# Perceiver cross-attention: 32x32 block transposes on VectorE and 32-row score products in place of 128x128 transposes on TensorE

## The chip, the cores and the metric

One core of one Trainium2 chip. The metric is the device time of one execution in microseconds (us); lower is better.

## The reference, cut to what matters

The program is a perceiver layer in three parts: cross-attention over a long context, a gated recurrence, and a mixture of eight experts. Only the first part and the loads at its end are touched.

```python
# x: (32, 64, 512) f32, ctx_1024: (32, 1601, 512) f32, d = 512
def _L0_xattn_ref(encoder_hc, decoder_hq, w_sim, b_sim, W_qv, b_qv):   # hc = layernorm(x), hq = ctx
    Sim = (hc @ w1)[:, :, None] + (hq @ w2)[:, None, :] + einsum('bid,bjd->bij', hc * w3, hq) + b_sim[0]
    hq_hat = einsum('bij,bjd->bid', softmax(Sim, axis=2), hq)
    Batt = softmax(max(Sim, axis=2), axis=1)
    hc_bar = einsum('bi,bid->bd', Batt, hc)[:, None, :]
    feats = concatenate([hc, hq_hat, hc * hq_hat, hc * hc_bar], axis=-1)
    return feats @ W_qv + b_qv
x = x + _L0_xattn_ref(_layernorm(x), ctx_1024, ...)
x = x + recurrence(...)      # unchanged
x = x + experts(...)         # unchanged
```

## The kernel before, in words

**Tiling.** The 32 batches go in 16 pairs; a pair's 2 x 64 query rows fill the 128 partitions. A batch's context has 1601 rows: 12 tiles of 128 and one of 65. Tiles 0 to 5 have two buffers (`ctx_two`, one of them lying in `x2`), tiles 6 to 12 one (`ctx_one`).

**Stages of a pair.** The normalised x (`tok_rows`) is turned on TensorE (L361) into `hcT`. VectorE makes the queries `qT = hcT * w3 + w2` (L619). Each context tile is turned by four 128x128 transposes on TensorE (`turn_ctx`, L353) into a PSUM bank T, batch 0's into T[0] and batch 1's into T[1]. ScalarE drains T[0] and VectorE T[1] into `ctxT` (`drain_ctx`, L487). The score product (`scores`, L390) contracts 128 features at a time in four steps, the batches on the two halves of the array's columns, into the PSUM banks S. VectorE takes each bank's maximum (L694), ScalarE the exponentials (L554). TensorE turns the probabilities (`turn_probs`, L371), and both engines drain them into `probsT`. The value product (L425) multiplies them with the untransposed context. Last comes the output product into Y: 12 matmuls with `hqhH/hqhL` (L396 to L398), 8 with `wb` and `hcT` (L458), 12 with `f2H/f2L`. VectorE adds Y to `xb` (L577). A side branch turns `tcol`, the row maxima (L417), makes the second softmax in one partition (L601 to L629), spreads it with one matmul (L431), and from it VectorE makes `hcb` (L637, L641); GpSimd then makes `wb` in four instructions (L327, L331).

**Order.** Every engine runs one `body(p, s, step)` a step (`steps`): the back half of pair p (values and output) with the front half of pair p + 1 (scores and softmax). On TensorE a body is: the 13 positions of the value product in `AV_ORDER`, with the first block of context transposes, the turn of `tok_rows` and that of `tcol` between them; the five score blocks of `BLOCKS`, the transposes of the next block put between the four contraction steps; the output product, with the turns of the probabilities in it. `turn_order` counts, for the waits, whose turn it is on T[0] and T[1].

```python
for c in range(C):                                              # scores, L384 to L391
    if j + 1 < NBLK and c < BLOCKS[j + 1][1]:
        turn_ctx(j + 1, 2 * c, p, fs, loads, step)
        turn_ctx(j + 1, 2 * c + 1, p, fs, loads, step)
    for b in range(2):
        last = pe.matmul(S[64 * b:64 * b + 64, k, col:col + w], qT[:, c, 64 * b:64 * b + 64],
                         buf[:, b, c, 0:w], start=(c == 0), stop=(c == C - 1))
```

**Queues.** SyncE issues all loads. In `step` it waits for each block of `ctx_one` to be read by the value product (`av_one`) and loads it again for the next pair (L241, L244), then stores the last x1 (L278), then loads x (L232) and both `ctx_two` blocks. GpSimd's `xb` (L318) waits for the store before last. ScalarE issues no DMA in this part.

An f32 matmul that is no transpose is two records in the trace, with two weight loads; an f32 transpose and an `fp32r` matmul are one.

Of the kernel before, what the change touches and what calls it, by code (L numbers as in the profile page):

```python
# [5 lines left out]
F32 = mybir.dt.float32  # L6
# [8 lines left out]
P = 128  # L15
# [28 lines left out]
BLOCKS = [(0, 3, 0, 0), (3, 3, 1, 0), (6, 3, 2, 0), (9, 2, 3, 0), (11, 2, 3, 256)]  # L44
NBLK = len(BLOCKS)
BANK_TILES = [(0, 3), (3, 3), (6, 3), (9, 4)]


TWO_SLOTS = 2
AV_ORDER = [t for j in [*range(TWO_SLOTS, NBLK), *range(TWO_SLOTS)] for t in range(BLOCKS[j][0], BLOCKS[j][0] + BLOCKS[j][1])]  # L50
AT_TILES = [(0, 4), (4, 3), (7, 3), (10, 3)]


def turn_order(front, back):

    bank = ([], [])
    for j, (_, n, _, _) in enumerate(BLOCKS):
        for u in range(2 * n if front else 0):
            bank[u % 2].append(f"ctx{j}.{u}")
    if front:  # L60
        bank[0].insert(1, "hc")
    if back:
        bank[1].insert(1 if front else 0, "trow")
# [30 lines left out]
def cross_attention(nc, sh, ident, x, ctx, w_sim, b_sim, W_qv, b_qv, x1, x2, ahead):  # L94
    D, C, JT, JMAIN, JTAIL, PAIRS = sh.D, sh.C, sh.JT, sh.JMAIN, sh.JTAIL, sh.PAIRS
    BW = 3 * P
    sems = []

    with ExitStack() as stack:
# [6 lines left out]

        TWO = BLOCKS[TWO_SLOTS][0]

        ctx_two = [[x2[:, b * TWO:(b + 1) * TWO, :] for b in range(2)], [sb(f"ctx_two{b}", [P, TWO, D]) for b in range(2)]]
        ctx_one = [sb(f"ctx_one{b}", [P, JT - TWO, D]) for b in range(2)]  # L110
        ctxT = [sb(f"ctxT{s}", [P, 2, C, BW]) for s in range(2)]
        w0, w3 = x2[:, 2 * TWO:2 * TWO + C, :], sb("w3", [P, C, D])
# [5 lines left out]
        qT = sb("qT", [P, C, P])  # L118
        probs = sb("probs", [P, JT * P])
        probsT = sb("probsT", [P, JT, P])  # L120
        hqhH, hqhL = sb("hqhH", [P, C, P], F32R), sb("hqhL", [P, C, P], F32R)
        wb = sb("wb", [P, 2, C, D])
        f2H, f2L = sb("f2H", [P, C, P], F32R), sb("f2L", [P, C, P], F32R)
# [10 lines left out]
        rstd = sb("rstd", [P, 1])  # L134
        mhalf = sb("mhalf", [P, 1])
        s1 = sb("s1", [P, 1])
        mx4 = sb("mx4", [P, 4])
        mx = sb("mx", [P, 1])
        nmx = sb("nmx", [P, 1])
        z4 = sb("z4", [P, 4])  # L140
# [9 lines left out]
        hcb = sb("hcb", [P, C, 2])  # L150

# [8 lines left out]
        hqhH_ready, hqhL_ready, f2H_ready = sem("hqhH_ready"), sem("hqhL_ready"), sem("f2H_ready")  # L160
        x_in = sem("x_in")
        ctx_in = [[sem(f"ctx_in{s}_{j}") for j in range(TWO_SLOTS)] for s in range(2)]
        ctx_one_in = [sem(f"ctx_one_in{j}") for j in range(TWO_SLOTS, NBLK)]
# [5 lines left out]
        rstd_ready = sem("rstd_ready")  # L169
        hc_ready = sem("hc_ready")  # L170
        xb_ready = sem("xb_ready")
        q_ready = sem("q_ready")
# [16 lines left out]
        f2_ready = sem("f2_ready")  # L189
# [3 lines left out]
        y_done = sem("y_done")  # L193
# [5 lines left out]
        def tile_rows(t):  # L199
            return P if t < JT - 1 else JTAIL  # L200

        def bank_cols(k):
            t0, n = BANK_TILES[k]
            return sum(tile_rows(t) for t in range(t0, t0 + n))

        def context(s, b, t):

            return (ctx_two[s][b], t) if t < TWO else (ctx_one[b], t - TWO)

        def block_dmas(j):  # L210
            t0, n, _, _ = BLOCKS[j]
            return 2 * (2 if t0 + n == JT else 1)

        def block_cols(j):
            t0, n, _, _ = BLOCKS[j]
            return sum(tile_rows(t) for t in range(t0, t0 + n))

        def steps(eng, body):

            body(-1, 0, "first")  # L220
            body(0, 0, "full")
            with eng.Fori(0, (PAIRS - 2) // 2) as i:
                body(2 * i + 1, 1, "full")
                body(2 * i + 2, 0, "full")
            body(PAIRS - 1, 1, "last")
# [4 lines left out]
        def _(sp):  # L230
# [3 lines left out]
            def load_block(j, s, pair):  # L234
                t0, n, _, _ = BLOCKS[j]
                done = ctx_in[s][j] if j < TWO_SLOTS else ctx_one_in[j - TWO_SLOTS]
                for b in range(2):
                    src = ctx[pair, b]
                    dst, i = context(s, b, t0)
                    full = min(n, JT - 1 - t0)  # L240
                    sp.dma_start(dst[:, i:i + full, :],  # L241
                                 src[0:JMAIN, :].rearrange("(p t) d -> p t d", t=JT - 1)[:, t0:t0 + full, :]).then_inc(done, 16)
                    if full < n:
                        sp.dma_start(dst[0:JTAIL, i + full, :], src[JMAIN:sh.J, :]).then_inc(done, 16)  # L244
# [8 lines left out]
            for j in range(NBLK):  # L253
                load_block(j, 0, 0)
# [9 lines left out]
            for j in range(TWO_SLOTS):  # L264
                load_block(j, 1, 1)

            def step(p, s, load, store):
                nxt = p + 1 if isinstance(p, int) else sp.snap(p + 1)
                if load:
                    ahead = p + 2 if isinstance(p, int) else sp.snap(p + 2)  # L270
                if store:
                    prev = p - 1 if isinstance(p, int) else sp.snap(p - 1)
                for j in range(TWO_SLOTS, NBLK):
                    sp.wait_ge(av_one, (NBLK - TWO_SLOTS) * p + j - TWO_SLOTS + 1)
                    load_block(j, None, nxt)
                if store:
                    sp.wait_ge(x1_ready, p)
                    sp.dma_start(x1[prev], xb[1 - s][:]).then_inc(x1_out, 16)  # L278
                if load:
                    sp.wait_ge(hc_ready, p + 2)  # L280
                    sp.wait_ge(xb_ready, p + 2)
                    load_x(ahead)
                    sp.wait_ge(av_done, p + 1)
                    for j in range(TWO_SLOTS):
                        load_block(j, s, ahead)
# [10 lines left out]
            ahead.load(sp)  # L296
# [7 lines left out]
        def _(pool):  # L304
            pool.memset(mhalf[:], -0.5).then_inc(consts, 1)
            pool.memset(ones1[:], 1.0).then_inc(consts, 1)
            pool.wait_ge(consts, 2)
            pool.wait_ge(const_in, 80)

            def body(p, s, step):  # L310

                if step != "last":
                    f = p + 1
                    pool.wait_ge(ln_ready, 2 * f + 2)
                    pool.tensor_tensor(rstd[:], ve[:], mhalf[:], ALU.pow).then_inc(rstd_ready, 1)  # L315
                    if not (isinstance(f, int) and f < 2):
                        pool.wait_ge(x1_out, 16 * (f - 1))
                    pool.tensor_tensor(xb[1 - s if step != "first" else 0][:], x_sb[:], bqv_b[:], ALU.add).then_inc(xb_ready, 1)  # L318
                if step != "first":
# [6 lines left out]
                    for b in range(2 if step == "full" else 0):  # L326
                        pool.tensor_tensor(wb[:, b], w3[:], hcb[:, :, b, None].to_broadcast([P, C, D]),  # L327
                                           ALU.mult).then_inc(wb_step, 1)
                    for b in range(2 if step == "full" else 0):
# [3 lines left out]
            steps(pool, body)  # L333

        @block.tensor
        def _(pe):
# [3 lines left out]

            def turn_ctx(j, u, p, fs, loads, step):

                t0, n, _, _ = BLOCKS[j]
                t, b, bank = t0 + u // 2, u % 2, u % 2
# [1857 lines left out]
```

## Time and profile before

| | |
|---|---|
| median of 3 runs | 1582.35 us (1582.21 to 1584.47) |
| span of the profiled execution | 1606.2 us |
| TensorE matmul busy | 1417.7 us, 88% |
| TensorE weight loads busy | 914.6 us, 57% |
| VectorE busy | 721.5 us, 45% |
| ScalarE busy | 377.6 us, 24% |
| GpSimd busy | 756.1 us, 47% |
| cross-attention | from the start to about 842 us |
| mean granted TensorE clock | 0.947 of 2.4 GHz |

The profiled execution has only its span: 1606.2 us from the first to the last instruction, 1.5% over the median of the unprofiled runs. Busy time of TensorE is the time covered by at least one matmul whose end is modelled, so matmuls that run side by side or pipelined count once. Shares of the whole span mix the three parts of the program; the cross-attention has to be read by itself.

### The profile page before, as it was taken

To read this page: it belongs to the slowest core of one execution; us is meant where nothing else is said; L and a number is where in the kernel's file an instruction comes from. 1 tells how busy PE (TensorE), PEld (TensorE's weight loads), DVE (VectorE), ACT (ScalarE), POOL (GpSimd) and SP (SyncE) were. 2 spreads that over 40 slices of the span, in tenths; PEclk is the share of its full clock that TensorE was granted. 3 is DMA by queue.
4 is the path that set the end of the run, shared out by engine and by line. 5 is a ranking of instruction groups with operands and counts; after the bars stand their busy time and mean duration, and the time that the engine had idled before them with its cause. 6 is when DMAs were issued, how large, how long until landed. Compare 5 with 4: busy or idle time off the path is not lost. (4 is left out here: it accounts for less than half of the span.)

```text
span 1606.2 us, 28597 instructions
## 1 busy us (share of the span) xinstructions
PE 1417.7 (88%) x9329; PEld 914.6 (57%) x9330; DVE 721.5 (45%) x1715; ACT 377.6 (24%) x716; POOL 756.1 (47%) x592
## 2 busy tenths in 40 slices
PE   5899999999999999999998777898549999996960
PEld 3455555555555555555546556666438888885750
DVE  2443434434344344443437776787583233231221
ACT  1322222322223222232215412222301111111110
POOL 0134431444214442144406855787495886806830
PEclk9999999999999999999998999999679999998985
DMA  9514542244422444224406569532103333314322
GB/s 331 191 53 147 177 177 92 107 154 176 172 96 99 162 176 161 107 92 169 170 7 224 165 242 318 176 111 97 66 27 131 137 137 131 139 57 144 117 67 103
DMA packets 94905, 225.10 MB, mean 140 GB/s; under 512 B 9448, under 2 KB 25960, under 8 KB 94864
## 3 DMA queue, kind: packets, MB, share of 16 engines
q1 hardware_dynamic: 85136, 191.02, 34.0%
q0 software_dynamic: 9200, 32.51, 5.8%
q10 hardware_dynamic: 528, 1.05, 0.2%
q8 instruction: 23, 0.38, 0.1%
q14 instruction: 18, 0.15, 0.0%
HBM read 179.20 MB, written 45.35 MB: 140 GB/s over the span
## 5 line engine op out<-in xcount | busy, mean ns | idle before, releaser
L487 DVE COPY ctxT<-T 128x512 f32<-128x512 f32 (+1 forms) x208 | 139.6, 671 | 251.4 <-PE T L353 251.4
L487 ACT COPY ctxT<-T 128x512 f32<-128x512 f32 (+1 forms) x208 | 118.7, 570 | 450.0 <-PE T L353 450.0
L390 PE MATMUL S<-ctxT,qT 128*64 128x384 f32 (+2 forms) x1280 | 211.7, 448 | 0.0
L318 POOL TENSOR_TENSOR xb<-x_sb,bqv_b 128x512 f32<-128x512 f32 x16 | 20.3, 1272 | 256.9 <-DMA x<-xb 256.9
L331 POOL TENSOR_TENSOR wb<-wb,x 128x2048 f32<-128x2048 f32 x30 | 135.5, 4538 | 0.0
L353 PEld LDWEIGHTS T<-ident,ctx_one 128*128 128x128 f32 (+1 forms) x896 | 92.0, 141 | 63.6 <-ACT ctxT L487 34.9
L315 POOL TENSOR_TENSOR rstd<-ve,mhalf 128x1 f32<-128x1 f32 x16 | 8.8, 551 | 252.7 <-DVE nmean L573 252.7
L353 PE MATMUL T<-ident,ctx_one 128*128 128x128 f32 (+1 forms) x896 | 116.9, 273 | 0.0
L327 POOL TENSOR_TENSOR wb<-w,hcb 128x2048 f32<-128x2048 f32 x30 | 107.5, 3606 | 19.1 <-DVE w12L L646 19.1
L1881 POOL TENSOR_TENSOR w_high<-w_low,f_zero 128x2048 fp32r<-128x2048 f32 x21 | 96.8, 4609 | 36.3 <-DMA w_low<-_L_ffn_gate_up_proj_dram 24.7
L1932 PE MATMUL f_Dn<-w_high,f_hH 128*128 x156 | 67.9, 435 | 49.6 <-issue 48.0
L425 PE MATMUL O<-ctx_one,probsT 128*64 128x512 f32 (+1 forms) x448 | 110.9, 611 | 0.0
L390 PEld LDWEIGHTS S<-ctxT,qT 128*64 128x64 f32 x1280 | 76.4, 136 | 57.4 <-issue 49.7
L1862 POOL TENSOR_TENSOR w_low<-w_low,w_high 128x2048 fp32r<-128x2048 f32 x21 | 96.7, 4606 | 1.6
L1398 PE MATMUL Pb<-WrT,yT 128*32 128x128 f32 x2016 | 71.8, 286 | 22.2 <-DVE yT L1633 20.1
L2037 DVE TENSOR_TENSOR f_hL<-f_TH,f_hH 128x512 fp32r<-128x512 f32 x39 | 27.0, 691 | 140.3 <-ACT f_hH L1987 140.3
L1992 ACT ACTIVATE sg<-f_G 128x512 f32<-128x512 f32 x39 | 23.4, 599 | 244.8 <-PE f_G L1934 212.6
L1398 PEld LDWEIGHTS Pb<-WrT,yT 128*32 128x32 f32 x2016 | 53.7, 113 | 33.4 <-DVE yT L1633 28.9
L353 PEld LDWEIGHTS T<-ident,x 128*128 128x128 f32 x384 | 45.1, 149 | 45.6 <-ACT ctxT L487 14.3
L353 PE MATMUL T<-ident,x 128*128 128x128 f32 x384 | 56.2, 293 | 16.5 <-DMA x<-in_ctx_dram 13.3
L458 PE MATMUL Y<-wb,hcT 128*64 128x512 f32 x256 | 65.1, 610 | 0.0
L1932 PE MATMUL f_U<-w_high,f_xH 128*128 x156 | 64.9, 416 | 0.0
(299 smaller groups left out, 2925.0 us busy)
## 6 DMA issues: line engine op xcount, KB each, us to landing
x<-in_ctx_dram SPq DMA_DIRECT2D x32, 768.0 KB, 7.3
ctx_one<-in_ctx_dram SPq DMA_DIRECT2D x32, 768.0 KB, 5.6
ctx_two<-in_ctx_dram SPq DMA_DIRECT2D x32, 768.0 KB, 7.3
ctx_one<-in_ctx_dram SPq DMA_DIRECT2D x32, 512.0 KB, 5.4
w_low<-_L_ffn_gate_up_proj_dram POOLq DMA_DIRECT2D x10, 1024.0 KB, 8.3
f_xt<-routed_x SPq DMA_DIRECT2D x39, 256.0 KB
routed_y<-f_yt SPq DMA_DIRECT2D x39, 256.0 KB
ctx_one<-in_ctx_dram SPq DMA_DIRECT2D x32, 256.0 KB
```

The lines of the kernel that those rows point to most:

```text
L327: pool.tensor_tensor(wb[:, b], w3[:], hcb[:, :, b, None].to_broadcast([P, C, D]), ALU.mult).then_inc(wb_step, 1)
L331: pool.tensor_tensor(wb[:, b], wb[:, b], w0, ALU.add).then_inc(wb_step, 1)
L353: last = pe.transpose(T[bank][:, c * P:c * P + rows], src[0:rows, i, c * P:(c + 1) * P], ident[0:rows, 0:rows])
L390: last = pe.matmul(S[64 * b:64 * b + 64, k, col:col + w], qT[:, c, 64 * b:64 * b + 64], buf[:, b, c, 0:w], start=(c == 0), stop=(c == C - 1))
L425: last = pe.matmul(O[64 * b:64 * b + 64, :], probsT[0:rows, t, 64 * b:64 * b + 64], src[0:rows, i, :], start=(n == 0), stop=(n == JT - 1))
L458: pe.matmul(Y[64 * b:64 * b + 64, :], hcT[s][:, c, 64 * b:64 * b + 64], wb[:, b, c, :], start=False, stop=False)
L487: copy(buf[:, bank, :, i * P:i * P + rows], T[bank][:].rearrange("p (c j) -> p c j", c=C)[:, :, 0:rows]).then_inc(t_free[bank], 1)
L1398: last = pe.matmul(Pb[o * B:(o + 1) * B, 0:P], src[:, c, prev, :], WrT[:, c, o * P:(o + 1) * P], start=(c == 0), stop=(c == C - 1))
L1862: pool.tensor_tensor(low, low.bitcast(F32), high[:, e % SLOTS, part].bitcast(F32), ALU.subtract).then_inc(w_parts, 1)
L1881: pool.tensor_tensor(high[:, e % SLOTS, part], ex.low[:, e % SLOTS, part].bitcast(F32), zero[:, None, :].to_broadcast([P, C, F]), ALU.add) ...
L1932: pe.matmul(bank[:], aH[:, c, :], high[:, slot, part, c, :], start=(c == 0), stop=False)
L2037: dve.tensor_tensor(hL[:], TH[:].rearrange("p (c i) -> p c i", c=C), hH[:].bitcast(F32), ALU.subtract).then_inc(hL_ready, 1)
```

## The change

What it does:

- The context transposes on TensorE, their drains and `ctxT` go. VectorE transposes the context from SBUF to SBUF in blocks of 32x32 (`dve.transpose`), two tiles of one batch an instruction, into `ctxA` (positions 0 to 3, later 9 to 12) and `ctxB` (4 to 8; its space also holds `probs`). Only the blocks are turned: partition group a (32 partitions) of the result holds, for each of 16 groups of 32 features, the features of tokens 32a to 32a + 31.
- A score matmul contracts 32 features: 16 steps k, for each batch the four partition groups a in turn, each with its own PSUM bank. It needs the queries with every feature group on all four partition groups (`qr`). ScalarE makes the queries into `f3`, writes them to DRAM (`q_rows`), waits, and reads them back in four DMAs.
- Three score blocks of 4, 5 and 4 positions in place of five. The row maximum is taken once at the end (three reductions), the exponentials in five instructions.
- The normalisation goes to ScalarE, at the end of the body before, and `hc` is turned ahead of the values. The two `f` operands share buffers (`hfH`, `hfL`). The output product's first 12 matmuls come ahead of the last score block.
- SyncE stores x1 first and loads x between the second and third part of `ctx_one`. The last two full bodies stand outside the loop. The load of `Wg` waits for the last scores.

```diff
+BLOCKS = [(0, 4, 0), (4, 5, 8), (9, 4, 4)]
+TAIL_POS = 8
+AV_ORDER = [*range(4, 13), *range(0, 4)]
+PARTS_ONE = [(4, 2, False), (6, 2, True), (8, 2, False), (10, 2, False)]
+PART_ENDS = [1, 4, 6, 8]
...
             def step(p, s, load, store):
...
+                    sp.wait_ge(x1_ready, p)
+                    sp.dma_start(x1[prev], xb[1 - s][:]).then_inc(x1_out, 16)
+                for i in range(len(PARTS_ONE)):
+                    if i == 2 and load:
+                        sp.wait_ge(hc_ready, p + 2)
+                        sp.wait_ge(xb_ready, p + 2)
+                        load_x(after)
+                    sp.wait_ge(av_one, len(PARTS_ONE) * p + i + 1)
+                    load_part(i, nxt)
                 if load:
                     sp.wait_ge(av_done, p + 1)
+                    load_two(s, after)
...
+            def scores(j, f):
+                t0, n, col = BLOCKS[j]
+                buf = (ctxA, ctxB)[j % 2]
+                pe.wait_ge(turned[j], f + 1)
                 if j == 0:
+                    pe.wait_ge(q_in, 64 * (f + 1))
+                    pe.wait_ge(exp_done, EXPS * f)
+                for k in range(DB):
+                    c, e = k // QUADS, k % QUADS
                     for b in range(2):
+                        for a in range(QUADS):
+                            w = n * Q
...
+                            last = pe.matmul(S[64 * b:64 * b + 64, a, col * Q:col * Q + w], qr[a * Q:(a + 1) * Q, e, c, 64 * b:64 * b + 64],
+                                             buf[a * Q:(a + 1) * Q, b, k, 0:w], start=(k == 0), stop=(k == DB - 1))
...
# body on TensorE, after the change: hc turn; values(p); scores(0); hqh turn; scores(1);
# 12 matmuls with hfH/hfL; scores(2); 8 with wb, turn_probs(0) in them; 12 with hfH/hfL, turn_probs(1 to 3) in them
...
# ScalarE, each body
+                    for c in range(C):
+                        act.activation(f3[:, c, :], hcT[fs][:, c, :], ACT.Identity, scale=w3T[:, c:c + 1],
+                                       bias=w2T[:, c:c + 1]).then_inc(q_made, 1)
+                    act.wait_ge(q_made, C * (f + 1))
+                    if later(f, 1):
+                        act.wait_ge(q_in, 64 * f)
+                    act.dma_start(q_d, f3[:].rearrange("p c i -> p (c i)")).then_inc(q_out, 16)
+                    act.wait_ge(q_out, 16 * (f + 1))
+                    if later(f, 1):
+                        act.wait_ge(qk_done, NBLK * f)
+                    for a in range(QUADS):
+                        act.dma_start(qr[a * Q:(a + 1) * Q].rearrange("p e c i -> p e (c i)"),
+                                      q_d.rearrange("(e r) d -> r e d", r=Q)).then_inc(q_in, 16)
...
# VectorE
+            def turn_two(buf, src, i, b, col):
+                return dve.transpose(buf[:, b, :, col * Q:(col + 2) * Q].rearrange("p k (t r) -> p t k r", r=Q),
+                                     src[:, i:i + 2, :].rearrange("p t (k r) -> p t k r", r=Q))
...
+            def row_max(f):
+                full, end = JTAIL // Q, (JT - 1) * Q
+                dve.wait_ge(qk_done, NBLK * (f + 1))
+                dve.tensor_reduce(mx3[:, 0:1], S[:, 0:full, 0:end + Q], axis=AX.XY, op=ALU.max).then_inc(mx_done, 1)
+                dve.tensor_reduce(mx3[:, 1:2], S[:, full:QUADS, 0:end], axis=AX.XY, op=ALU.max).then_inc(mx_done, 1)
+                dve.tensor_reduce(mx3[:, 2:3], S[:, full, end:end + JTAIL % Q], axis=AX.X, op=ALU.max).then_inc(mx_done, 1)
...
# VectorE's body after the change: add_x; second softmax; f3, hcb (wait q_out); s1; turn_second;
# norm_stats; hqhL; f3; turn_third; hfL; row_max; tcol; half of turn_first for the next pair;
# drain_probs 0 and 2; the other half of turn_first; zsum, rz
```

## Rows read from the trace of the kernel before

**Rows 1.** The page: the span, and the busy time and share of the engines.
```profile
span 1606.2 us, 28597 instructions
PE 1417.7 (88%) x9329; PEld 914.6 (57%) x9330; DVE 721.5 (45%) x1715; ACT 377.6 (24%) x716; POOL 756.1 (47%) x592
```

**Rows 2.** Windows: busy us (instructions) of PE, PEld, DVE, ACT, POOL; clock, DMA share, GB/s.
```profile
57.00:815.60 758.60, 755.93 (x4495) 399.85 (x4494) 315.26 (x701) 202.89 (x421) 268.27 (x89) 1.00 0.39 140
262.00:312.40 50.40, 50.37 (x303) 26.72 (x302) 20.85 (x48) 13.48 (x29) 17.93 (x6) 1.00 0.38 141
281.00:291.00 10.00, 10.00 (x68) 5.54 (x66) 3.84 (x6) 3.52 (x6) 10.00 (x3) 1.00 0.89 338
```

**Rows 3.** Timeline, PE: start us, us; the value product's start in two bodies, and others.
```profile
261.98 1.08 PE L425 MATMUL O<-ctx_one,probsT 128*64 128x512 f32 x4
...
264.70 1.09 PE L353 MATMUL T<-ident,ctx_two 128*128 128x128 f32 x8
265.72 1.08 PE L425 MATMUL O<-ctx_one,probsT 128*64 128x512 f32 x4
...
267.75 3.66 PE L425 MATMUL O<-ctx_one,probsT 128*64 128x512 f32 x16
...
312.38 1.08 PE L425 MATMUL O<-ctx_one,probsT 128*64 128x512 f32 x4
```

**Rows 4.** Groups of PE, busy us, mean ns: one body's (262.0 to 312.4); L390's, the page's.
```profile
L458 PE MATMUL Y<-wb,hcT 128*64 128x512 f32 x16 | 4.1, 611 | 0.0
L371 PE MATMUL T<-ident,probs 128*128 128x128 f32 x12 | 2.1, 287 | 0.0
L390 PE MATMUL S<-ctxT,qT 128*64 128x384 f32 (+2 forms) x1280 | 211.7, 448 | 0.0
```

**Rows 5.** Timeline, PE: 32 matmuls of the recurrence, four column groups of the array in turn.
```profile
1000.32 1.08 PE L1398 MATMUL Pb<-WrT,yT 128*32 128x128 f32 x32
```

**Rows 6.** Groups of DVE by form: the recurrence's block transpose; one body's copy and reductions.
```profile
L1633 DVE STREAM_TRANSPOSE yT<-H 128x128 f32<-128x128 f32 x64 | 19.9, 311 | 2.2
L487 DVE COPY ctxT<-T 128x512 f32<-128x512 f32 x12 | 8.3, 692 | 14.9 <-PE T L353 14.9
L694 DVE TENSOR_REDUCE mx<-S 128x1 f32<-128x384 f32 x3 | 1.6, 547 | 0.0
```

**Rows 7.** Groups of ACT by form in the same body.
```profile
L554 ACT ACTIVATE probs<-S,nmx 128x384 f32<-128x384 f32 x3 | 1.7, 578 | 0.4 <-DVE nmx L676 0.4
L554 ACT ACTIVATION_READ_ACCUMULATOR probs<-S,nmx 128x1 f32 x4 | 0.8, 203 | 0.0
L522 ACT ACTIVATE erow<-erow 1x128 f32<-1x128 f32 x1 | 0.3, 303 | 0.0
```

**Rows 8.** DMA issues: count, KB each, median us from issue to landing; one issue's length.
```profile
x_sb<-in_x_dram SPq DMA_DIRECT2D x16, 256.0 KB, 2.6
x<-xb SPq DMA_DIRECT2D x16, 256.0 KB, 5.8
...
281.08 0.33 SPq L232 DMA_DIRECT2D x_sb<-in_x_dram  x1
```

**Rows 9.** Timeline, POOL, in the same body.
```profile
280.81 7.17 POOL L327 TENSOR_TENSOR wb<-w,hcb 128x2048 f32<-128x2048 f32 x2
287.94 9.03 POOL L331 TENSOR_TENSOR wb<-wb,x 128x2048 f32<-128x2048 f32 x2
```

**Rows 10.** Timeline, PE, in the last body; [idle before <-what ended it].
```profile
828.65 0.66 PE L361 MATMUL T<-ident,tok_rows 128*128 128x128 f32 x4 [0.79 <-ACT tok_rows L535]
830.80 0.76 PE L396 MATMUL Y<-w12H,hqhH 128*128 128x512 f32 x1 [1.49 <-DVE hqhL L667]
...
832.21 0.63 PE L396 MATMUL Y<-w12H,hqhH 128*128 128x512 f32 x1
832.64 0.63 PE L397 MATMUL Y<-w12L,hqhH 128*128 128x512 f32 x1
```

**Rows 11.** Timeline, PE, at the start: first score product and first value product.
```profile
25.25 1.55 PE L390 MATMUL S<-ctxT,qT 128*64 128x384 f32 x4
...
57.03 1.97 PE L425 MATMUL O<-ctx_one,probsT 128*64 128x512 f32 x4
```

More of the change, by code:

```diff
@@ L197, in first, with tile_rows, context, part_dmas @@
             return isinstance(p, int) and p == 0
[L199 to L225, printed above, removed]
+        def tile_rows(pos):
+            return JTAIL if pos == TAIL_POS else P
+        def context(s, b, pos):
+            if pos < TWO:
+                return ctx_two[s][b], pos
+            if pos == TAIL_POS:
+                return ctx_one[b], ONE - 1
+            return ctx_one[b], pos - TWO - (pos > TAIL_POS)
+        def part_dmas(i):
+            return 2 * (2 if PARTS_ONE[i][2] else 1)
+        def bodies(eng, body):
+            body(-1, 0, "first", 1)
+            body(0, 0, "full", 2)
+            with eng.Fori(0, (PAIRS - 4) // 2) as i:
+                body(2 * i + 1, 1, "full", i + 2)
+                body(2 * i + 2, 0, "full", i + 3)
+            body(PAIRS - 3, 1, "full", PAIRS // 2)
+            body(PAIRS - 2, 0, "full", None)
+            body(PAIRS - 1, 1, "last", None)
         block = stack.enter_context(nc.Block())
@@ new lines, in values @@
+            def values(p, s, step):
+                pe.wait_ge(hqh_ready, p)
+                for n, pos in enumerate(AV_ORDER):
+                    for q in range(len(AT_TILES)):
+                        if AT_TILES[q][0] == n:
+                            pe.wait_ge(t_free[q % 2], turn(q % 2, f"probs{q}", *before(p)) + 1)
+                    if n == 1:
+                        pe.wait_ge(tcol_ready, p + 1)
+                        fill(1, "trow", p, step)
+                        pe.transpose(T[1][0:1, 0:P], tcol[:], ident[:]).then_inc(t_full[1], 1)
+                    for b in range(2):
+                        rows = tile_rows(pos)
+                        src, i = context(s, b, pos)
+                        last = pe.matmul(O[64 * b:64 * b + 64, :], probsT[0:rows, n, 64 * b:64 * b + 64],
@@ L512, in body @@
                 if front:
-                    drain_ctx(act, copy, 0, 0, p, fs, step, only=(0,))
                     act.wait_ge(t_full[0], turn(0, "hc", p, step) + 1)
@@ L560, in _ @@
+            act.wait_ge(const_in, 80)
+            norm(0)
+            bodies(act, body)
         @block.vector
@@ new lines, in turn_second @@
+            def turn_second(f):
+                dve.wait_ge(ctx_one_in[0], 16 * part_dmas(0) * (f + 1))
+                for b in range(2):
+                    turn_two(ctxB, ctx_one[b], 0, b, 0)
+                dve.wait_ge(ctx_one_in[1], 16 * part_dmas(1) * (f + 1))
+                for b in range(2):
+                    turn_two(ctxB, ctx_one[b], 2, b, 2)
+                for b in range(2):
+                    op = dve.transpose(ctxB[0:96, b, :, 4 * Q:5 * Q], ctx_one[b][0:96, ONE - 1, :].rearrange("p (k r) -> p k r", r=Q))
+                op.then_inc(turned[1], 1)
@@ L656, in body @@
                 if front:
[L657 to L661 removed]
+                    turn_second(f)
+                if loads is not None:
+                    norm_stats(f + 1)
                 if back:
                     dve.wait_ge(hqhH_ready, p + 1)
[L665 removed]
```

446 lines of the change are left out of this document (204 added, 242 removed).

## The prediction, made before the changed kernel had run

> **What bounds the kernel now.** I read the page first [rows 1]: TensorE is busy 88% of the span, but that mixes three parts of the program. The windows are next [rows 2]: from 57 to 815.6 us TensorE is busy 755.9 of 758.6 us at full granted clock (2.4 GHz), while VectorE has 42% and GpSimd 35%. The DMA engines have 39%, and move 338 GB/s at 89% where they work. Then the timeline for the period: the value product starts at 261.98 and again at 312.38 [rows 3], so a body takes 50.4 us, and fifteen start at that pace. In this part only fewer or denser TensorE instructions make the time shorter, until something else takes over.
>
> What fills 50.4 us: the transposes at L353 come eight a time; eight begin at 264.70 and the values resume at 265.72 [rows 3], so one costs 1.02 / 8 = 0.128 us with its share of the switch to and fro. There are 13 tiles x 4 x 2 = 104: **13.3 us**. Scores: 211.7 us in 16 pairs [rows 4] = **13.2 us**. Values: 16 records (4 positions) in 3.66 - 0.2 us of modelled tail = 3.46 [rows 3], so 13 positions take 11.3 us. The L458 products take 4.1 and the turned probabilities 2.1 [rows 4]. The remainder, 50.4 - 13.3 - 13.2 - 11.3 - 4.1 - 2.1 = 6.4 us, is the 24 `fp32r` matmuls and the small turns.
>
> **Part by part.** *Transposes on TensorE*: gone, -13.3 us a body. Their drains (26 copies, up to 0.69 us [rows 6]) were beside them and are worth nothing by themselves.
>
> *Scores.* The columns streamed stay the same if the four partition groups stream at once: 16 steps of 416 columns against 4 steps of 1601. The present product costs 13.2 us with its switches to transposes. From the recurrence: 32 records of 128 columns, four column groups, in 1.08 us [rows 5]; less the 0.27 us of the last one's tail, 0.81 / 8 = 0.10 us a round of four. Its four tiles differ in columns; the new product has eight tiles, four partition groups by two halves of the columns, of which no row shows the partition groups. If all eight go together, a round of 128 columns costs 0.10 to 0.11 us whoever is in it; 16 steps x 2 records x 0.109 x 416/128 = **11.3 us**. Bounds: 11 us below (nothing streams the columns faster), 4 x 11.3 = 45 us above (partition groups one after another). I take the lower end, because the nearest row shows four tiles in the time of one.
>
> The Trainium skill ("TensorE: Matmul & The Clock Gate", Part 3) gives four row tiles of 512 columns as 3.07 times one, not 4; by that the scores would be 45 / 3.07 = 14.7 us, an estimate, and the body 3.4 us longer than I say. No row here shows it.
>
> *Context on VectorE.* One block transpose of 128 elements takes 0.311 us [rows 6]; a copy of 512 takes 0.69. On the line through these, 0.99 ns an element over 0.18 us, 1024 elements cost 1.20 us and 512 cost 0.69. Twelve and two of them: 15.8 us a body. Bounds: half of it, if SBUF to SBUF ran at twice the pace (8 us), and double, if the scattered output cost as much again (32 us, which would put VectorE near 43 us and make it the bound); I take the line, since one of its two rows is the same operation. VectorE has 20.9 us a body now [rows 2]; the drains (9) and the queries (1.1) go, so 27 us with the new small ones: covered, if it is not late.
>
> *Row maximum and exponentials.* Today three of four banks are reduced while scores run. After: 1248 elements on the same line (1.4 us), 384 (0.55 us [rows 6]), and three small ones with their waits: 2.6 us after the last score. ScalarE's first exponential then takes 0.7 with 0.2 for the accumulator [rows 7]. TensorE has only six of the eight L458 matmuls (3.1 us) to put beside these 3.6 us, then waits on the third and fourth exponential. I put **+1.5 us** on the path (0.5 to 3).
>
> *Queries through DRAM.* With the values' start at 0: `hcT` copied at 1.2, second softmax's exponential at 2.9, four activations by the 0.303 us row [rows 7] to 4.1, the write's issue 0.33 [rows 8], its landing between 2.6 and 5.8 us later (the two 256 KB rows [rows 8]), then four issues one behind the other (1.4 us) and 1 MB of reads: 2.6 us at best, more behind the `ctx_one` parts that SyncE issues from 2.5 us on. At 338 GB/s [rows 2] 1 MB alone is 3.1 us. So `qr` is full between 11 and 21 us; TensorE wants it after the values and two small turns, at 12.5. I take 15: **+2.5 us** (0 to 8). ScalarE is blocked meanwhile; behind it stands only the scaling of O, due at 12.5. VectorE's wait for `q_out` holds `hcb` to about 9 us: GpSimd's chain of 7.17 + 9.03 us [rows 9] ends at 25.5, and its product is wanted near 30: hidden, with 5 us to spare.
>
> *VectorE's order.* `turn_second` runs 9.5 to 16, with `hqhL` at 20.5 behind the turn of `tok_rows` after the first score block, `turn_third` to 26; TensorE reaches the third block at 27. Free, barely; each us on VectorE beyond that comes onto the path.
>
> *Ends of the body.* The normalisation (0.7 us) now follows the last drain on ScalarE: **+0.6 us** before `hc` is turned. SyncE's x load waits for `xb`, that for the x1 store (5.8 us [rows 8]): parts 3 and 4 start near 9.5 and land by 18, wanted at 21. The moved store, load of Wg and unrolled bodies: nothing, 15 us and more of slack or the same work.
>
> *Clock.* After idle stretches of 0.79 and 1.49 us in the last body, an `fp32r` matmul starts 0.43 us behind the one before it [rows 10], against at most 6.4 / 24 = 0.27 in the full bodies: the lower level, 1.2 GHz, for some 3 us. The new wait of 2.5 us can bring that on in each body: **+1 us** (0 to 3).
>
> Sum: 50.4 - 13.3 - (13.2 - 11.3) = 35.2, + 1.5 + 2.5 + 0.6 + 1 = 40.8; with 1.2 us for switches between the 32-row tiles and the rest (0 to 2; bound by the switch share above) **42 us a body**, 8.4 saved, times 15 = 126 us. *Start*: the first score comes at 25.25, the first value at 57.03 [rows 11], 32 us; after, two transposed parts and 11.3 us of scores, tied to VectorE's 15.8 us and the landing context, end near 45: 12 us saved. 1606.2 - 138 = 1468 of the profiled span. That span is 1.5% above the median; times 0.985 it is **1446 us**.
>
> **Rivals.** *(A) The forecast*, 37 to 45 us a body: 1372 to 1490. *(B) The queries come 5 us later still* (small packets beside 4 KB ones): 47 us a body, 1520. For it, the 5.8 us row; against, the DMA engines stand idle half the body. *(C) Matmuls never start denser than in the densest stretch of this trace*, 0.81 / 31 = 0.026 us apart [rows 5]: 768 records x 0.026 = 20 us; the body is 50 us and only the start gains: 1570, within 30 either way. For it: no stretch here is denser. Against: there the streaming of the columns explains the pace fully. By a sentence of the same page (Part 1) starts never come closer than 25 ns, which would make the scores 19.2 us; the row at 26 ns neither refutes nor needs it. *(D) The slower side: partition groups of one half of the columns stream one after another.* Scores cost up to 45 us, the body 34 longer less the waits it covers (some 4): 72 us. 1606.2 + 15 x 21.6 - 12 = 1918, times 0.985 = 1890. It decides from scores of about 20 us on, less than two groups at once. For it: only column groups are seen together in the trace, and two records of the same product must follow each other; against: the groups have their own partitions and PSUM banks, and one batch's four are issued together. *(E) VectorE the bound* at doubled transposes is inside B's time or C's.
>
> **Numbers.** A 0.55, B 0.12, C 0.13, D 0.20 (its milder forms included). A and B are faster; C falls to faster 0.06, same 0.03, slower 0.04. So faster 0.73, same 0.03, slower 0.24. 0.2%, about 3 us, is what a measurement of this kernel can tell from no change. The range takes in A, B and the faster half of C: 1370 to 1585; what is left out is D above. A's own is 1372 to 1490.
>
> **What would show it.** Right: value products start 40 to 44 us apart; L353 gone; each score block busy near 3.5, 4.4, 3.5 us; block transposes near 1.20 us; before the first score block a wait for `qr`'s DMA of 2 to 3 us; a wait of TensorE on `probs` near 1 us. Wrong: score blocks of 6 us (C) or 14 us (D); block transposes of 2 us; a wait for `qr` over 6 us (B); `wb` as a releaser.

## The result, and the profile after

The change makes the kernel slower: 1719.43 us (median of 4, 1715.72 to 1721.39) against 1582.28 us beside it, a ratio of 1.0868 (95% interval 1.0849 to 1.0887). The forecast was 1446 us, range 1370 to 1585: the sign and the range were both missed.

The page of the changed kernel, against [rows 1]; under it its transposes, its DMA queues and its issues.

```profile
span 1716.9 us, 46419 instructions
PE 1246.2 (73%) x18673; PEld 884.3 (52%) x18674; DVE 860.1 (50%) x1619; ACT 301.2 (18%) x636; POOL 767.4 (45%) x610
q10 hardware_dynamic: 12048, 22.03, 4.3%
q8 instruction: 135, 2.21, 0.5%
L393 PE MATMUL S<-ctxA,x 32*64 32x128 f32 x8192 | 166.3, 317 | 256.5 <-DMA x<-q_rows 172.4
L593 DVE STREAM_TRANSPOSE ctxA<-ctx_one 128x1024 f32<-128x1024 f32 x64 | 73.9, 1212 | 13.7 <-PE S L393 13.7
ctx_one<-in_ctx_dram SPq DMA_DIRECT2D x128, 512.0 KB, 9.7
x<-q_rows ACTq DMA_DIRECT2D x64, 256.0 KB, 11.0
```

TensorE did what was asked: 1246 us busy where it had 1418. But it has gone from 88% to 73% of its span, and one wait stands out, that of L393 for the queries read back from DRAM. The instruction queue q8 moved 135 packets; in the kernel before, its line reads "q8 instruction: 23, 0.38, 0.1%".

The windows of one body, against the middle line of [rows 2]: values, the stretch behind them, the rest.

```profile
429.60:441.50 11.90, 11.90 (x56) 3.83 (x55) 4.85 (x9) 2.43 (x6) 2.79 (x2) 1.00 0.76 255
441.50:455.40 13.90, 0.39 (x2) 0.00 (x0) 9.32 (x12) 0.69 (x1) 13.90 (x4) 0.70 1.04 323
455.40:488.00 32.60, 28.06 (x829) 21.91 (x829) 15.65 (x22) 5.58 (x16) 1.80 (x3) 0.92 0.08 31
```

TensorE is idle for the whole middle stretch, with the DMA engines full. The timeline of PE, of the same body, against [rows 3]:

```profile
429.59 1.08 PE L417 MATMUL O<-ctx_one,probsT 128*64 128x512 f32 x4
...
438.29 3.60 PE L417 MATMUL O<-x,probsT 128*64 128x512 f32 x16
455.42 1.99 PE L393 MATMUL S<-ctxA,x 32*64 32x128 f32 x61 [13.53 <-DMA x<-q_rows]
...
467.29 2.16 PE L393 MATMUL S<-ctxB,x 32*64 32x129 f32 x115 [1.59 <-issue]
...
472.33 4.09 PE L393 MATMUL S<-ctxA,x 32*64 32x128 f32 x256
477.89 2.79 PE L460 MATMUL Y<-wb,hcT 128*64 128x512 f32 x12 [1.48 <-issue]
...
488.00 1.08 PE L417 MATMUL O<-ctx_one,probsT 128*64 128x512 f32 x4
```

The value products of the sixteen pairs start from 71.5 to 953.8 us, so a body takes 882.3 / 15 = 58.8 us; before, from 57.0 [rows 11] at 50.6. That is 14.5 us at the start and 15 x 8.25 = 123.7 us after it, 138 in all: the whole loss (137) lies in the attention. (The two profiled spans differ by 111 us only: from the last pair's value product to the end the trace before has 791 us and the trace after 763, the difference that chips show below.) Below, a body is always this mean over fifteen, and a block's time runs from its first matmul's start to its last one's, as a mean over fourteen bodies. A wait before a block is counted from the start of the matmul before it, so that some 0.5 us of it is that matmul itself; in the rows, the time in brackets is idleness alone. The three score blocks take 6.0, 6.4 and 4.8 us, 17.3 in place of 11.3, and block 0 starts 26.7 us after the values where the forecast's terms give 12.5 + 2.5 + 0.6 = 15.6. 11 + 6 = 17 us is the gap between 58.8 and the forecast 42.

Where the queries lose their time: ScalarE's timeline, then the group of transfers of `q_rows` in this body, then the DMA of 442 to 453 us.

```profile
431.75 1.63 ACT L517 ACTIVATE f<-hcT,w2T,w3T 128x128 f32<-128x128 f32 x4
433.49 0.35 ACTq L522 DMA_DIRECT2D q_rows<-f  x1
438.56 1.91 ACTq L527 DMA_DIRECT2D x<-q_rows  x4
```
```profile
DMA to landing us min/median/max: 5.0/9.8/15.4
```
```profile
q1 hardware_dynamic: 630, 2.44, 72.4%
q10 hardware_dynamic: 532, 0.99, 31.9%
```

The write leaves 3.9 us after the values start, as forecast (4.1), and needs 5.0 us, inside its bounds. The reads are issued from 9.0 us on, and the last lands 15.4 us after its issue. The third fence says why: SyncE's queue q1, which has ten context transfers of 6 MB under way, and ScalarE's q10 get through nearly as many packets (630 and 532), but q1's hold 3.9 KB and q10's 1.9 KB, so 72% of the bytes are context. The queries' megabyte moves at 90 GB/s. The Trainium skill ("DMA: Bandwidth & Descriptors", Queues, rings and completion order) says that a DMA engine goes round its queues packet by packet; the counts of packets in this window agree with that.

### The profile page after: what moved, and what is told of

Its sections match the earlier page's. It is cut to its first block and busy times, and to the rows that moved or that the text cites. A ratio compares the mean times of both kernels' runs of the same rounds, so it can differ in the third digit from the quotient of the medians.

```text
span 1716.9 us, 46419 instructions
## 1 busy us (share of the span) xinstructions
PE 1246.2 (73%) x18673; PEld 884.3 (52%) x18674; DVE 860.1 (50%) x1619; ACT 301.2 (18%) x636; POOL 767.4 (45%) x610
## 5 line engine op out<-in xcount | busy, mean ns | idle before, releaser
L393 PE MATMUL S<-ctxA,x 32*64 32x128 f32 x8192 | 166.3, 317 | 256.5 <-DMA x<-q_rows 172.4
L393 PEld LDWEIGHTS S<-ctxA,x 32*64 32x64 f32 x8192 | 151.3, 155 | 282.5 <-issue 281.9
L417 PE MATMUL O<-ctx_one,probsT 128*64 128x512 f32 (+1 forms) x576 | 135.8, 606 | 0.0
L393 PE MATMUL S<-ctxB,x 32*64 32x160 f32 (+2 forms) x4096 | 83.4, 296 | 26.1 <-issue 26.1
L393 PEld LDWEIGHTS S<-ctxB,x 32*64 32x64 f32 x4096 | 70.5, 132 | 37.0 <-issue 36.8
L593 DVE STREAM_TRANSPOSE ctxA<-ctx_one 128x1024 f32<-128x1024 f32 x64 | 73.9, 1212 | 13.7 <-PE S L393 13.7
L593 DVE STREAM_TRANSPOSE ctxB<-ctx_one 128x1024 f32<-128x1024 f32 x64 | 73.8, 1207 | 0.0
L417 PEld LDWEIGHTS O<-ctx_one,probsT 128*64 128x64 f32 (+1 forms) x576 | 37.3, 137 | 62.4 <-issue 58.6
L551 ACT ACTIVATE ctxB<-S,nmx 128x512 f32<-128x512 f32 (+2 forms) x80 | 41.0, 528 | 146.1 <-DVE nmx L639 146.1
L1976 PE MATMUL f_Dn<-w_low,f_hH 128*128 x156 | 62.7, 402 | 0.0
## 6 DMA issues: line engine op xcount, KB each, us to landing
x<-in_ctx_dram SPq DMA_DIRECT2D x16, 1024.0 KB, 15.4
```

What stands on the lines that cost most here:

```text
L393: last = pe.matmul(S[64 * b:64 * b + 64, a, col * Q:col * Q + w], qr[a * Q:(a + 1) * Q, e, c, 64 * b:64 * b + 64], buf[a * Q:(a + 1) * Q, ...
L417: last = pe.matmul(O[64 * b:64 * b + 64, :], probsT[0:rows, n, 64 * b:64 * b + 64], src[0:rows, i, :], start=(n == 0), stop=(n == JT - 1))
L593: return dve.transpose(buf[:, b, :, col * Q:(col + 2) * Q].rearrange("p k (t r) -> p t k r", r=Q), src[:, i:i + 2, :].rearrange("p t (k r) ...
L1976: pe.matmul(bank[:], aH[:, c, :], ex.low[:, slot, part, c, :], start=False, stop=False)
```

## The experiments

Chips differ: the kernel before took 1606 us on the chip of the first four runs, 1604 on that of the next four, 1582 on that of the last three. Ratios are to it on the same chip. The difference lies behind the attention: from the last value product on, the eight kernels of the first two chips take 782 to 792 us, the three of the last one 762 to 766, as the changed kernel's first trace does (763). So the bodies may be compared across chips; the changed kernel's takes 58.8 us in one trace and 59.2 in `again`.

**hold.** Parts 2 to 4 of `ctx_one` and x are loaded only when the queries have landed.

```diff
-                    if i == 2 and load:
+                    if i == 1 and load:
                         sp.wait_ge(hc_ready, p + 2)
+                        sp.wait_ge(q_seen, p + 2)
                         sp.wait_ge(xb_ready, p + 2)
...
+                    act.wait_ge(q_in, 64 * (f + 1))      # ScalarE, behind its four reads
+                    act.sem_inc(q_seen, 1)
```


> The changed kernel, but SyncE loads x and the second, third and fourth part of ctx_one only after the queries' four reads have landed (ScalarE waits for them and signals). Theory T1 (the reads are late because they share the DMA engines with the context loads: 15 us of landing against 3 to 4 alone): qr is full about 13 us after the values start, TensorE's wait before the first score block falls from 13.5 us to under 2, the body from 59 to 46 to 48 us, the time to about 1550. Rival R1 (the round trip is long by itself: a chain of write, wait, four issues and reads): the reads still end past 20 us, the body stays over 54 us, the time over 1640.

Measured: ratio 1.0533 (1.0513 to 1.0554), 1691.75 us, a body of 55.2 us: neither side's forecast of the whole holds. The queries' last packet comes 14.5 us after the values' start, not 25.6, and block 0's wait falls from 15 to 3.7 us. PE's timeline of a body whose values start at 404.20:

```profile
419.22 5.61 PE L394 MATMUL S<-ctxA,x 32*64 32x128 f32 x256 [2.72 <-DMA x<-q_rows]
424.76 0.66 PE L366 MATMUL T<-ident,tok_rows 128*128 128x128 f32 x4
430.00 5.09 PE L394 MATMUL S<-ctxB,x 32*64 32x160 f32 x141 [4.59 <-DVE ctxB L619]
```

So some 11 of the 15 us are the sharing. But 11 us earlier queries gave back only 3.6 us a body: block 1 now waits 5.6 us for the context that was held, and the blocks themselves grew to 19.0 us. With `hold`, 14.5 us is what the round trip costs with the engines nearly to itself: the forecast's 15 was the price of an undisturbed trip.

**local.** No DRAM: ScalarE and VectorE each copy eight 32x512 pieces of `f3` to the four partition groups of `qr`.

```diff
-                    act.dma_start(q_d, f3[:].rearrange("p c i -> p (c i)")).then_inc(q_out, 16)
...
-                        act.dma_start(qr[a * Q:(a + 1) * Q].rearrange("p e c i -> p e (c i)"),
-                                      q_d.rearrange("(e r) d -> r e d", r=Q)).then_inc(q_in, 16)
+                    for e in range(2):                    # VectorE: e in range(2, 4)
+                        for a in range(QUADS):
+                            act.copy(qr[a * Q:(a + 1) * Q, e], f3[e * Q:(e + 1) * Q]).then_inc(q_in, 1)
```


> The changed kernel, but the queries don't go through DRAM: ScalarE and VectorE copy f3 onto the four partition groups of qr in eight 32-row copies each. T1: no DMA before the first score block; its wait under 1 us; the low clock after it gone, so the first block takes 5 us instead of 6.3; the body 45 to 47 us; the time about 1525. Rival R2 (VectorE, with 5 us of copies more, becomes the bound): the body 52 us or more, TensorE waiting for the block transposes before the second or third score block.

Measured: 1561.7 us, ratio 0.9731 (0.9714 to 0.9749), faster than the kernel before. A body takes 47.3 us, a little over the 45 to 47 expected, and block 0 isn't waited for (0.5 us, the matmul before it). Everything else in the change stays. But the blocks take 18.3 us (5 us were expected of the first, it takes 5.7), though nothing delays block 0 and block 1 waits only 1.6 us for its operands.

**order.** The column halves of one partition group are issued in turn, not the four groups of one half.

```diff
-                    for b in range(2):
-                        for a in range(QUADS):
+                    for a in range(QUADS):
+                        for b in range(2):
```


> The changed kernel with the two inner loops of the score product swapped: the partition groups outside, the batches inside. Theory T3 (all eight tiles of a step go together whatever their order, as the trace after shows eight starts in 50 ns and then 109 ns to the next eight): the same within 5 us. Rival R3 (the order decides which tiles overlap): score blocks longer or shorter by over 1 us each, the time by over 20 us either way.

Measured: ratio 1.0973 (1.0947 to 1.1), a body of 59.1 us, blocks 6.1, 6.3 and 5.1 us. The body is that of `again` below (59.2 us), but it was profiled in the fastest of the four runs. The ratio is above both of the unedited kernel's (1.0868, and 1.0903 in `again`) by more than the intervals, 11 to 17 us; no unedited run stands beside it on this chip. So the new order gains nothing, the traces show no block longer or shorter by 1 us, and whether it costs up to 1 us a body stays open.

**half.** Scores over 8 of the 16 feature groups; half of the contraction is left out (the last step kept closes the sum).

```diff
-                for k in range(DB):
+                for k in range(DB // 2):
```


> The changed kernel with only 8 of the 16 feature groups in the score product (half of the contraction is left out). Theory T2 (the score blocks take 17 us a body instead of 11.3 because instructions come too slowly, in 16 KB fetches every 3.6 us, now that the loop is too long to stay where it is held): per matmul the supply stays the bound, if the loop of some 160 KB is still fetched each time: blocks of 3.1, 3.3 and 2.5 us, fetches go on. If the shorter loop is held, no fetches in the loop and blocks at the streaming pace: 1.8, 2.2 and 1.8 us. Rival R4 (the blocks are slow for another reason, the clock or the tiles): half the time of the present blocks whether fetches are there or not.

```profile
q8 instruction: 87, 1.43, 0.4%
```

Measured: 1616.02 us (one run), a body of 50.7 us. The blocks take 3.3, 2.4 and 1.8 us, 7.6 in all, less than half of 17.3, near the forecast's pace of 1.8, 2.2 and 1.8 but for block 0, whose rounds all run at half clock (213 ns). The wait for the queries stays at 15.5 us. The instruction packets go on, about 5 a body (57 from 250 to 850 us), some 3.9 us apart in the scores. The expectation tied the streaming pace to packets that are gone; here both come together, so packets as such don't cost. A block is now 256 TensorE instructions, about one packet's worth, and in fourteen bodies a single gap is left in the blocks, of 0.65 us.

**again.** The changed kernel unedited, on the chip of the next three.

> The changed kernel once more, nothing edited, as the yardstick of the kernels beside it. Every theory expects the ratio of the first timing within its interval, 1.085 to 1.089, 58.8 us a body, and block 0 waiting about 15 us for its queries.

Measured: ratio 1.0903 (1.0866 to 1.094), overlapping the first timing's interval, a body of 59.2 us, block 0's wait 15.1 us.

**early.** `local`, with the product that makes `s1` ahead of the one that releases GpSimd.

```diff
+                        score_bias(f)                    # the tensor_tensor_reduce into s1
+                        dve.wait_ge(s1_ready, f + 1)
                     dve.tensor_tensor(f3[:], hcT[s][:], Y[:, None, 0:P]
...
-                    dve.tensor_tensor_reduce(out=f3[:]..., accum_out=s1[:]).then_inc(s1_ready, 1)
```


> The kernel with local query copies, and in it VectorE's product with two SBUF operands that makes s1 moved ahead of the product that releases GpSimd, so that GpSimd is idle while it runs. T4 (such an instruction doesn't end while GpSimd works: it took 4.06 us beside GpSimd's first product against 0.68 us in the kernel before): it takes 0.7 us again, the transposes of block 1 begin and end about 3.4 us earlier, block 1's gap of 1.7 us behind block 0 is gone, and a body takes 1.5 to 3 us less than 47.3, so 1510 to 1540 us on this chip. R5 (the 4 us are the instruction's own, for its operands' places or its form in the changed kernel): it still takes 4 us, GpSimd starts 4 us later, and a body takes 47.3 us or up to 3 more.

The product's group in `local` and in `early` (VectorE, all sixteen):

```profile
L690 DVE CUSTOM_DVE_ANT_0 f<-tok_rows,w_b 128x512 f32<-128x512 f32 x16 | 58.2, 3635 | 2.6 <-DVE hcb L679 2.6
```
```profile
L653 DVE CUSTOM_DVE_ANT_0 f<-tok_rows,w_b 128x512 f32<-128x512 f32 x16 | 11.1, 692 | 26.3 <-ACT x L525 26.1 <-DVE x L644 0.2
```

The instruction's 3.4 us were GpSimd's, as expected; the body's gain was not. It takes 47.4 us, the ratio is 0.9715 (0.970 to 0.973) against 0.9731 for `local`: no difference that the intervals show. Block 1's operands are there 3.5 us sooner, its gap is gone, and the time reappears inside block 1 (8.7 us after 7.9). PE in a body of `early`:

```profile
359.74 2.39 PE L394 MATMUL S<-ctxA,x 32*64 32x128 f32 x146
363.64 1.86 PE L394 MATMUL S<-ctxA,x 32*64 32x128 f32 x110 [1.51 <-issue]
365.43 0.66 PE L366 MATMUL T<-ident,tok_rows 128*128 128x128 f32 x4
366.01 0.51 PE L394 MATMUL S<-ctxB,x 32*64 32x160 f32 x13
369.94 6.19 PE L394 MATMUL S<-ctxB,x 32*64 32x129 f32 x243 [3.41 <-issue]
```

"<-issue" is idle time for which no semaphore answers. The DMA records have an instruction packet of 16 KB that starts at 361.30 and one at 367.45, each beside such a gap.

**narrow.** All but the first feature group write half of their columns; the instructions stay.

```diff
+                            w = w // 2 if k else w
```


> Of the score products all but those of the first feature group write only half of their columns (64 in place of 128, 16 in place of 32): half of the sum is left out of the other columns; the number of instructions stays. T2 (blocks are bound by the supply of TensorE's instructions, 8.3 ns each, and by gaps beside the fetches): the three blocks take nearly what they took, 5.5, 6.0 and 4.5 us or at most 1 us less, fetches as many as before. R6 (streaming of columns bounds them): they fall to half, near 3.2, 3.3 and 2.5 us.

Measured: 1756.07 us (one run; `again` beside it 1748.66), a body of 60.1 us. The blocks take 5.8, 5.7 and 5.2 us, 16.7 in place of 17.4, for nearly half of the streaming. Block 2 of one body, where the changed kernel has one row of 4.09 us:

```profile
479.76 1.70 PE L394 MATMUL S<-ctxA,x 32*64 32x128 f32 x129
482.64 1.58 PE L394 MATMUL S<-ctxA,x 32*64 32x64 f32 x127 [1.19 <-issue]
```

The clock differs too. The windows of this body, block 0 with the start of block 1, and block 2 (the clock is the third number from the end):

```profile
464.20:472.00 7.80, 6.49 (x288) 5.86 (x292) 0.01 (x1) 0.59 (x1) 0.92 (x3) 0.50 0.22 87
479.70:484.30 4.60, 3.34 (x257) 3.13 (x257) 0.73 (x2) 0.62 (x1) 0.00 (x0) 1.00 0.03 7
```

Block 0 runs at half clock to its end, where the changed kernel is back at the full one before its end (from 461.0 us on, in the body shown above); rounds of 64 columns at half clock take about the 109 ns of 128 at the full one, so block 0 says nothing on columns, nor does the start of block 1. Block 2 does: at full clock in both, it takes 5.2 us against 4.8 to 5.0. Its rounds of eight take 90 ns in the mean in place of 109 to 115, and rounds over 0.5 us (gaps, below) grow in all blocks from 2.9 to 5.1 us a body: what is saved in streaming is waited for instead. The count of instructions sets this block's time, not its columns.

**quarter.** Scores over 4 of the 16 feature groups (three quarters of the contraction left out).

```diff
-                for k in range(DB):
+                for k in range(DB // 4):
```


> Scores over 4 of the 16 feature groups, three quarters of the contraction left out: the pair of bodies that the loop holds shrinks to about the instruction count that it had in the kernel before the change. T5 (the gaps come from fetches of TensorE's instructions, which begin when the loop's two bodies no longer stay loaded): no instruction packets in the steady stretch of the loop, the whole run near the 23 of the kernel before, and the three blocks take at most 1.6, 1.1 and 1.0 us. R7 (fetches belong to any loop with the new scores): still some 30 to 50 instruction packets in the loop. The wait of block 0 for its queries stays at about 15 us with both.

```profile
q8 instruction: 28, 0.46, 0.1%
```

Measured: 1564.29 us (one run), a body of 47.7 us, blocks 1.6, 1.7 and 1.0 us, no gap over 0.5 us in them. In the loop the packets are gone: 28 on the page, none between 196 and 707 us. Block 1 was expected at 1.1: most of its rounds run at half clock. The wait for the queries is 14.8 us.

**flat** (the kernel before) and **flatq** (`quarter`): TensorE's loop written out, the other engines' kept.

```diff
-            with pe.Fori(0, (PAIRS - 2) // 2) as i:
+            for i in range((PAIRS - 2) // 2):
```


> The kernel before the change, with TensorE's loop over the pairs written out body by body (the other engines keep theirs), so that every 16 KB of TensorE's instructions is fetched once and nothing of the loop is reused. T6 (a fetch is served every 3.6 us, and stalls TensorE only where 256 instructions are used up in less than that): a body of this kernel holds 600 matmuls and weight loads in 50 us, one fetch per 21 us, so some 40 more instruction packets and a ratio between 0.998 and 1.005. R8 (every fetch stops TensorE for the 1.1 to 1.9 us of the gaps seen in the changed kernel): 2.3 fetches a body, 3 to 4 us more for each of 14 bodies, ratio 1.025 to 1.04.

> The kernel with a quarter of the feature groups, TensorE's loop written out: 600 to 800 instructions a body, all of them fetched. T6: three fetches a body, with dense stretches of 128 instructions only, so the three blocks stay at 1.6, 1.7 and 1.0 us within 1 us in all, and a body at 47.8 us. R8: each body 3 to 5 us longer.

Measured: `flat` has 52 packets on its page for 23 (29 more, 40 were expected), and the ratio 0.9988 (0.9977 to 1.0). `flatq` has 52 for 28, a body of 48.0 us (47.7 in `quarter`), blocks 4.4 us (4.3). A fetch every 20 us costs nothing; the fetches as such aren't the loss.

**spread.** `early`, with block 1 behind the twelve products into Y.

> The kernel with local copies and the early s1, and in it block 1 of the scores put behind the twelve products into Y that came after it, so that block 0 and block 1 are parted by 3.6 us of slow instructions and block 1 meets fewer of the context loads. T6 (block 1 stalls about 3 us at its start because a fetch comes late beside the context loads): the stall shrinks below 1.5 us, a body takes 46 to 47.2 us in place of 47.6, 1535 to 1555 us. R9 (the stall belongs to the count of instructions, and moves along with them): the gaps of the three blocks add up to the same, a body takes 47.6 us or up to 1.5 more, since TensorE waits for the products' operands.

Measured: ratio 0.9752 (0.9733 to 0.9772) against 0.9715 (0.970 to 0.973), a body of 47.8 us against 47.4. Block 1 falls from 8.7 to 5.7 us, block 2 rises from 4.8 to 7.1, and block 0 stays near 6: together 18.7 us (19.8 in `early`), with 5.5 us of gaps (5.7). The gaps moved with the instructions, as the second theory said; the gain expected of the first did not come. (The median, 1542.68 us, lies in the first one's range only because this chip is 1.4% faster than the one that the range was made for.)

**What the blocks' 17.3 us are.** In the changed kernel, by the matmuls' starts: 19 of 32 rounds of block 0 at 213 ns or more instead of 109, 2.0 us; gaps (rounds of eight over 0.5 us), 2.9 us; the rest is streaming (11.3) and 1.1 us of uneven rounds. The half clock, and the full one in block 2 (windows of the same kind):

```profile
455.40:459.40 4.00, 3.98 (x145) 3.99 (x146) 0.00 (x0) 0.00 (x0) 1.80 (x3) 0.50 0.53 219
472.30:476.30 4.00, 4.00 (x257) 3.70 (x256) 0.69 (x1) 0.62 (x1) 0.00 (x0) 1.00 0.01 4
```

The first comes right behind the 13.5 us of idleness. The gaps come in the stretches with the instruction packets, of which the scores of this body (455.4 to 476.5 us) have:

```profile
q8 instruction: 6, 0.10, 1.8%
```

They start at 457.26, 460.79, 464.31, 468.38, 471.97 and 475.45 us, 3.5 to 4.1 us apart, though each takes only 0.9 to 1.4 us. `narrow`'s follow at the same distance (465.80, 469.30, 472.65, 476.46, 480.02, 483.79). A body has 885 matmuls and 884 loads and 7.7 packets (79 from 250 to 850 us), so 16 KB are some 230 of them; in `flat` 605 and 2.5. At a packet per 3.6 us, the blocks' 1536 instructions would need 24 us if none lay ready; the kernels with all 768 matmuls a body show 16.7 to 19.8 us, whatever their columns, order or start. That the number of instructions in a streak sets the gaps, and not the columns, is shown by block 2 of `narrow` and by `half` and `quarter`, whose gaps are gone. That TensorE waits there for its packets is argued: no semaphore answers, and the packets follow each other at a fixed distance while the gaps come. The match isn't one to one: beside 17 of the 29 idle gaps over 0.5 us of the changed kernel's fourteen bodies no packet is under way (beside 4 of 39 in `early`). Why a packet comes only each 3.6 us, and how many lie ready, stays open.

## Why the prediction was wrong, step by step

**Queries through DRAM: the step that failed most.** "`qr` is full between 11 and 21 us ... I take 15: +2.5 us (0 to 8)." It came at 25.6. Block 0 starts 26.7 us after the values, and 12.4 in `local`: the round trip cost 14.4 us a body, where 2.5 were put. The times up to the reads' issue were right. The reads were priced as one megabyte beside idle engines ("against, the DMA engines stand idle half the body" in rival B), but in just this stretch 6 MB of context go first or alongside: 338 GB/s [rows 2] over 7 MB is 21 us, and the share goes by packets. The row needed was there, in the 0.89 share of the window. B was the right rival with the wrong size: it put 47 us a body for queries 5 us later, and they came 10.6 later.

**Scores, 11.3 us.** The mechanism held: eight tiles do stream at once, rounds of eight records at 109 ns in block 2, 4.09 us for its 256 records with the 0.27 us tail. So C and D are out: starts are down to 7 ns apart (472.814, .821, .827 us), denser than C's 26, and the figures of 3.07 and 25 ns from the Trainium skill ("TensorE: Matmul & The Clock Gate", Parts 3 and 1) aren't seen in these products. C came near all the same (20 us for 17.3, by the count of records), for another reason than its own: the starts can be dense, but not for long. What is missing in the sum is a term for the supply of instructions: 885 matmul records a body in place of 303. No row of the kernel before could price it, since its loop fetched nothing; that the trace was silent was no reason for nothing, and a count of instructions would have shown it to be the one resource that tripled.

**Clock, +1 us (0 to 3).** The mechanism and, at 2.0 us, nearly the size; the wait that brings it was six times what was put.

**Start, 12 us saved.** It lost 14.5. The first score comes at 37.2 us where it was 25.25 [rows 11], again for the queries (`local`: 23.9), and then the first scores take 24.8 us with gaps of 1.2 to 2.8 us. `local` has its first value product at 62.2, not at 45: without the trip through DRAM the start still loses 5 us, where 12 were to be saved.

**VectorE.** The block transposes cost 1.212 us and 0.66 against 1.20 and 0.69: right within 0.03. VectorE has 29.8 us a body, not 27: 3.4 of it is the `s1` product beside GpSimd, which no step had. **Row maximum**: 1.02, 0.95 and small ones, 2.4 us for 2.6. The forecast had the wrong pieces (1248 and 384 elements; they are 832 and 768), and the sum fits by luck, since both pairs come to about 1600; TensorE's waits on the probabilities are at most 0.6 us, where 1.5 was put. **GpSimd's chain** ends at 26.9 us for 25.5, and is not waited for.

**What the gain was.** With the round trip taken away, as in `local`, the change does pay: fewer TensorE microseconds for VectorE's spare ones. In the changed kernel this was given back, some 14 us a body before the scores and 6 within. The 6 within are still there in `local`; the kernels without them, `half` and `quarter`, leave out part of the contraction, so that a full product can have them back isn't shown.

## What to carry to other kernels

When a transfer is put on the path, price it in the very window where it will run, by what is queued on the other queues then and by the size of packets, not by an average share; 32-partition operands can be copied between partition groups by ScalarE and VectorE in 5 us, with no DRAM. When an edit multiplies the instructions of a dense stretch, count them per body and compare with what the loop holds. Past that, supply can become a bound that neither busy time nor streamed columns show: here it did with blocks of 512 instructions, and not with blocks of 256. Look for gaps "<-issue" and for the instruction queue's packets.

## What the runs showed of the hardware

- A loop of two bodies of 605 TensorE instructions was fetched once and not again (no instruction packet from 205 to 831 us in the kernel before, none from 196 to 707 us in `quarter`); one of two bodies of 1769 is fetched all over each time, and so is one of two bodies of 1001 (`half`). The Trainium skill ("Runtime: NRT & Kernel Launch", Instruction fetch mechanics) describes a FIFO refilled in blocks of 16 KiB, and calls the cost of crossing a block mostly hidden. The runs agree where matmuls are sparse (`flat`: a packet each 20 us, ratio 0.9988) or dense blocks short (`half`); in the full score blocks 2.9 us of gaps a body are left. The short loops moved no packet at all, which a FIFO alone doesn't tell.
- A VectorE instruction with two SBUF inputs that starts 0.09 us behind a GpSimd instruction on a tensor ends 0.54 us behind that instruction's end: 4.05 us for 0.68. VectorE's and GpSimd's timelines in the changed kernel (the second row is two instructions, of 3.60 and 4.05 us):

```profile
440.07 4.05 DVE L681 CUSTOM_DVE_ANT_0 f<-tok_rows,w_b 128x512 f32<-128x512 f32 x1 [0.17 <-DVE hcb L672]
```
```profile
439.98 7.61 POOL L343 TENSOR_TENSOR wb<-w,hcb 128x2048 f32<-128x2048 f32 x2 [6.73 <-DVE hcb L672]
```

  The block transposes beside the same GpSimd work keep their 1.2 us. The Trainium skill ("SBUF — State Buffer", SBUF: two separate sides) calls the shared pair of ports an exclusive lock, held for a whole instruction; `local` and `early` agree. GpSimd's second instruction pays too: 4.05 us in the changed kernel and `local`, 3.60 in `early` and in the kernel before.
- Eight tiles of the array (four partition groups by two column halves) take 109 ns for eight records of 128 columns in block 2; a transpose of 128 columns over the whole array took 128 ns in the kernel before, with its switches.
